# A retrieval-and-dense kernel: the product of M and Wo in three fp32r passes instead of fp32, later, with its operands split on chip

## The reference

```python
x = L0_attn_hidden_states                      # (8, 256, 512) = 16 tiles of 128 rows
xn = _layernorm(x, axis=-1)
# attention part, H 32 heads, HKV 8, D 128, G = H // HKV = 4
q = (xn @ Wq.T + bq).reshape(b, s, H, D)
sig_q = jax.nn.elu(q) + 1.0
q_sel = sig_q[:, :, ::G, :]                    # 8 of the 32 heads
num = einsum('bshd,hde->bshe', q_sel, M)
den = einsum('bshd,hd->bsh', q_sel, z)[..., None] + EPS
out_heads = jnp.repeat(num / den, G, axis=2)
output = out_heads.reshape(b, s, H * D) @ Wo.T
# dense part
out = einsum('bsd,df->bsf', xn, w.astype(float32) * w_scale) + b
x = x + output + out
```

## Time and profile before

| | |
|---|---|
| runs | 243.65 to 243.77 us, median 243.72 |
| profiled execution | 243.56 us, its span from first to last instruction 241.7 us |
| PE busy (matmuls) | 234.1 us, 97% |
| DVE, ACT, POOL busy | 178.0, 119.6, 108.4 us |
| granted clock of PE | full in all slices |
| P's products | from 57.9 to 81.8 us |

### The profile page before, as it was taken

The page is one execution under the profiler, slowest core; times in us unless marked ns, Lnnn a source line. Parts: engine busy times, 40 slices in busy tenths (PEclk is TensorE's granted clock), DMA queues, the critical chain, the costliest instruction groups (busy, mean ns, idle before and its releaser), DMA issues.

```text
span 241.7 us, 3385 instructions
## 1 busy us (share of the span) xinstructions
PE 234.1 (97%) x1030; PEld 186.7 (77%) x1030; DVE 178.0 (74%) x266; ACT 119.6 (49%) x276; POOL 108.4 (45%) x108
## 2 busy tenths in 40 slices
PE   8699999998999999999999999999999999999995
PEld 2488788885776788888888888888888888788885
DVE  2889695897998669887687694958666778995631
ACT  2654626628648923655463526455463747341110
POOL 1058734756271815553434326263403629657500
PEclk9999999999999999999999999999999999999999
DMA  7999999999370211424252515221212223244441
GB/s 225 405 417 411 383 242 225 216 217 217 94 252 5 53 51 52 127 54 126 53 168 53 161 50 169 52 91 42 88 52 73 56 75 108 76 136 136 133 174 44
DMA packets 21985, 34.83 MB, mean 144 GB/s; under 512 B 5200, under 2 KB 13136, under 8 KB 20816
## 3 DMA queue, kind: packets, MB, share of 16 engines
q1 hardware_dynamic: 19344, 26.63, 33.4%
q0 software_dynamic: 1376, 6.82, 13.4%
q10 hardware_dynamic: 1248, 1.18, 1.8%
HBM read 22.02 MB, written 4.19 MB: 108 GB/s over the span
## 4 chain that ended last, share of the span: by engine, by line
PE 33%; issue 31%; POOL 18%; DVE 8%; SPq 4%; DMA 2%; ACT 2%; ACTq 1%; POOLq 0%; DVEq 0%
POOL e_and_sz L313 9%; POOL xT L288 5%; PE attn_ps L793 4%; PE attn_ps L794 4%; PE attn_ps L795 4%; SPq L219 4%; POOL x L321 3%; PE q_ps L793 3%; PE q_ps L795 3%; PE q_ps L794 3%; DVE aT_lo L654 2%; PE dense_ps L793 2%; PE dense_ps L795 2%; PE dense_ps L794 2%; DMA xT<-in_xT 2%
## 5 line engine op out<-in xcount | busy, mean ns | idle before, releaser
L313 POOL TENSOR_TENSOR e_and_sz<-s,z_b 128x512 f32<-128x512 f32 x32 | 42.0, 1340 | 40.3 <-DVE den L633 40.2
L441 ACT ACTIVATE s<-s,rden 128x128 f32<-128x128 f32 x128 | 39.2, 389 | 40.5 <-DVE rden L637 40.5
L793 PE MATMUL attn_ps<-P_hi,aT_hi 128*128 128x512 f32 (+1 forms) x128 | 49.8, 389 | 0.5 <-DVE aT_lo L654 0.5
L795 PE MATMUL attn_ps<-P_hi,aT_lo 128*128 128x512 f32 (+1 forms) x128 | 49.1, 383 | 0.0
L794 PE MATMUL attn_ps<-P_lo,aT_hi 128*128 128x512 f32 (+1 forms) x128 | 49.0, 383 | 0.0
L793 PE MATMUL q_ps<-WqT_hi,xT_hi 128*128 128x512 f32 x104 | 42.1, 405 | 0.3 <-DVE s L628 0.3
L795 PE MATMUL q_ps<-WqT_hi,xT_lo 128*128 128x512 f32 x104 | 40.6, 390 | 0.0
L794 PE MATMUL q_ps<-WqT_lo,xT_hi 128*128 128x512 f32 x104 | 40.5, 389 | 0.0
L288 POOL TENSOR_TENSOR xT<-xT,mean_b 128x512 f32<-128x512 f32 x13 | 18.3, 1408 | 37.8 <-ACT mean_b L390 31.2
L621 DVE SCALAR_TENSOR_TENSOR q_ps<-q_ps,rstd,bq_b 128x512 f32<-128x512 f32 x28 | 21.0, 753 | 19.3 <-PE q_ps L795 19.3
L793 PEld LDWEIGHTS attn_ps<-P_hi,aT_hi 128*128 128x128 f32 x128 | 24.1, 188 | 6.2 <-issue 0.9
(11 more groups left out here) (82 smaller groups left out, 365.3 us busy)
## 6 DMA issues: line engine op xcount, KB each, us to landing
x<-in_WoT POOLq DMA_DIRECT2D x6, 1024.0 KB, 10.6
x<-in_x SPq DMA_DIRECT2D x16, 256.0 KB, 3.9
xT<-in_xT SPq DMA_DIRECT2D x16, 256.0 KB, 4.1
aT<-s SPq DMA_DIRECT2D x124, 32.0 KB, 1.9
out<-x SPq DMA_DIRECT2D x15, 256.0 KB, 2.3
MT<-s SPq DMA_DIRECT2D x96, 32.0 KB, 1.9
x<-in_WoT SPq DMA_DIRECT2D x2, 1024.0 KB, 14.0
s<-in_WqT SPq DMA_DIRECT2D x2, 512.0 KB, 7.1
```

The source lines that it names most:

```text
L313: nc.gpsimd.tensor_tensor(sz_eps[:, :, h * D // 2:(h + 1) * D // 2].rearrange("p g (j c) -> p j g c", j=2), by_quarter(sbuf_s[:, t % SRING ...
L441: last = nc.scalar.activation(a_g, a_g, ACT.Copy, scale=rden[:, t % 2, g:g + 1])
L793: nc.tensor.matmul(out, x_hi, w_hi, start=start, stop=False)
L795: return nc.tensor.matmul(out, x_lo, w_hi, start=False, stop=stop)
```

## The change

- P(g) becomes three fp32r passes. M (`MT`, 128x1024) and the eight 128x512 parts of the sum of Wo get a high part, made by ACT (`copy_M_hi`, `copy_Wo_hi(g)`), and a low part, made by DVE (`split_M_lo`, `split_Wo_lo(g)`). No space is added: M's parts lie in the second buffers of aT_hi and aT_lo, Wo's where P_hi and P_lo come to lie.
- P(g) waits for M_lo and Wo_lo(g) in place of the loads.
- PE's list: after q(5,1) now mean(7), dense(5), q(6,0), P(0), P(1), q(6,1), P(2), P(3), dense(6), P(4), mean(8); from there on unchanged.
- DVE and ACT get the new operations into their lists; the copies and splits of P, the denominators of tiles 2 and 3, the turns of tiles 1 and 3 and make_a(3) come later in them.

```diff
--- before.py
+++ after.py
@@ -85,6 +85,10 @@
         sz_eps = e_and_sz[:, E:].rearrange("p (g d) -> p g d", g=G)
         w_f32 = e_and_sz[:, 0:K * HID].rearrange("p (k n) -> p k n", n=HID)
         Wo_sum = x[:, FIRST_LENT:, :]
+        MT_hi = aT_hi[:, 1, :, :]
+        MT_lo = aT_lo[:, 1, :, :]
+        Wo_hi = P_hi
+        Wo_lo = P_lo
 
         q_ps = [bank(f"q{i}_ps") for i in range(4)]
         dense_ps = bank("dense_ps")
@@ -127,6 +131,10 @@
         wd_by_dve = sem("wd_by_dve")
         wd_hi_ready = sem("wd_hi_ready")
         wd_lo_ready = sem("wd_lo_ready")
+        M_hi_ready = sem("M_hi_ready")
+        M_lo_ready = sem("M_lo_ready")
+        Wo_hi_ready = sem("Wo_hi_ready")
+        Wo_lo_ready = sem("Wo_lo_ready")
         P_filled = sem("P_filled")
         P_hi_ready = sem("P_hi_ready")
         P_lo_ready = sem("P_lo_ready")
@@ -429,6 +437,14 @@
                 act.wait_ge(qneg_ready, 2 * t + h + 1)
                 nc.scalar.activation(e, e, ACT.Exp, scale=-1.0).then_inc(exp_ready, 1)
 
+            def copy_M_hi():
+                act.wait_ge(M_in, 16)
+                nc.scalar.activation(MT_hi, MT[:], ACT.Copy).then_inc(M_hi_ready, 1)
+
+            def copy_Wo_hi(g):
+                act.wait_ge(wo_added[g // GJ], 16 * (R - 1))
+                nc.scalar.activation(Wo_hi[:, g, :], Wo_sum[:, g, :], ACT.Copy).then_inc(Wo_hi_ready, 1)
+
             def copy_P_hi(g):
                 act.wait_ge(P_filled, g + 1)
                 nc.scalar.activation(P_hi[:, g, :], attn_ps[g % 2][:], ACT.Copy).then_inc(P_hi_ready, 1)
@@ -500,31 +516,38 @@
             copy_xT_hi(6)
             exp_of(4, 1)
             make_a(1)
+            copy_M_hi()
             exp_of(5, 0)
+            exp_of(5, 1)
+            copy_mean(7)
+            for g in range(GJ):
+                copy_Wo_hi(g)
+            exp_of(6, 0)
             copy_P_hi(0)
-            exp_of(5, 1)
             copy_P_hi(1)
-            copy_mean(7)
-            exp_of(6, 0)
+            copy_Wo_hi(4)
+            copy_Wo_hi(5)
+            copy_xT_hi(7)
+            exp_of(6, 1)
             copy_P_hi(2)
-            copy_xT_hi(7)
             copy_P_hi(3)
-            exp_of(6, 1)
+            copy_Wo_hi(6)
+            copy_Wo_hi(7)
+            copy_mean(8)
             copy_P_hi(4)
             copy_aT_hi(0)
+            copy_P_hi(5)
             make_a(2)
-            copy_mean(8)
-            copy_P_hi(5)
-            make_a(3)
             for t in range(LEAD, T):
                 exp_of(t, 0)
+                if t == LEAD:
+                    copy_P_hi(6)
+                    copy_P_hi(7)
                 if t + 1 < T:
                     copy_xT_hi(t + 1)
-                if t == LEAD:
-                    copy_P_hi(6)
                 exp_of(t, 1)
                 if t == LEAD:
-                    copy_P_hi(7)
+                    make_a(3)
                 copy_aT_hi(t - LEAD + 1)
                 if t + 2 < T:
                     copy_mean(t + 2)
@@ -606,6 +629,15 @@
                 dve.wait_ge(wd_hi_ready, j + 1)
                 nc.vector.tensor_tensor(wd_lo[:, ks, :], wd_raw[:, ks, :], wd_hi[:, ks, :].bitcast(F32), ALU.subtract
                                         ).then_inc(wd_lo_ready, 1)
+
+            def split_M_lo():
+                dve.wait_ge(M_hi_ready, 1)
+                nc.vector.tensor_tensor(MT_lo, MT[:], MT_hi.bitcast(F32), ALU.subtract).then_inc(M_lo_ready, 1)
+
+            def split_Wo_lo(g):
+                dve.wait_ge(Wo_hi_ready, g + 1)
+                nc.vector.tensor_tensor(Wo_lo[:, g, :], Wo_sum[:, g, :], Wo_hi[:, g, :].bitcast(F32), ALU.subtract
+                                        ).then_inc(Wo_lo_ready, 1)
 
             def split_P_lo(g):
                 dve.wait_ge(P_hi_ready, g + 1)
@@ -727,39 +759,46 @@
             add_dense(4)
             add_bias(5, 1)
             make_s(5, 0)
+            split_M_lo()
+            make_s(5, 1)
+            add_dense(5)
+            split_Wo_lo(0)
+            split_Wo_lo(1)
+            add_bias(6, 0)
+            turn_blocks(1)
+            split_Wo_lo(2)
+            split_Wo_lo(3)
+            make_s(6, 0)
             split_P_lo(0)
-            make_s(5, 1)
-            add_bias(6, 0)
             split_P_lo(1)
-            turn_blocks(1)
-            add_dense(5)
+            split_xT_lo(7)
+            add_bias(6, 1)
+            split_Wo_lo(4)
+            split_Wo_lo(5)
+            moments(8)
+            split_P_lo(2)
+            make_s(6, 1)
+            split_P_lo(3)
+            split_Wo_lo(6)
+            split_Wo_lo(7)
+            add_dense(6)
             denominator(2)
-            split_P_lo(2)
-            make_s(6, 0)
-            add_bias(6, 1)
-            split_xT_lo(7)
-            split_P_lo(3)
-            moments(8)
-            denominator(3)
-            add_dense(6)
-            make_s(6, 1)
             split_P_lo(4)
             split_aT_lo(0)
+            split_P_lo(5)
             turn_blocks(2)
             for t in range(LEAD, T):
                 add_bias(t, 0)
-                if t == LEAD:
-                    split_P_lo(5)
                 if t + 2 < T:
                     moments(t + 2)
                 add_bias(t, 1)
                 if t == LEAD:
                     split_P_lo(6)
-                if t == LEAD:
                     split_P_lo(7)
-                turn_blocks(t - BEHIND - 1)
+                    denominator(3)
                 if t == LEAD:
                     split_xT_lo(t + 1)
+                turn_blocks(t - BEHIND - 1)
                 make_s(t, 0)
                 if LEAD < t < T - 1:
                     split_xT_lo(t + 1)
@@ -847,14 +886,14 @@
 
             def product_P(g):
                 if g == 0:
-                    pe.wait_ge(M_in, 16)
-                pe.wait_ge(wo_added[g // GJ], 16 * (R - 1))
+                    pe.wait_ge(M_lo_ready, 1)
+                pe.wait_ge(Wo_lo_ready, g + 1)
                 if g < 2:
                     pe.wait_ge(s_ready, 9 + g)
                 else:
                     pe.wait_ge(P_lo_ready, g - 1)
-                nc.tensor.matmul(attn_ps[g % 2][:], MT[:, g, :], Wo_sum[:, g, :], start=True, stop=True
-                                 ).then_inc(P_filled, 1)
+                three_passes(attn_ps[g % 2][:], MT_hi[:, g, :], MT_lo[:, g, :], Wo_hi[:, g, :], Wo_lo[:, g, :], True, True
+                             ).then_inc(P_filled, 1)
 
             def product_attn(t):
                 if t == 0:
@@ -935,13 +974,13 @@
             product_q(5, 0)
             product_dense(4)
             product_q(5, 1)
-            product_P(0)
-            product_q(6, 0)
-            product_P(1)
             spread_mean(7)
             product_dense(5)
+            product_q(6, 0)
+            product_P(0)
+            product_P(1)
+            product_q(6, 1)
             product_P(2)
-            product_q(6, 1)
             product_P(3)
             product_dense(6)
             product_P(4)
```

## The result

The changed kernel takes 249.55 us (median of 4 runs, 249.25 to 249.99) against 243.69 for the kernel before: 1.0241 of its time, 95% interval 1.0226 to 1.0256. The profiled execution took 249.74 us with a span of 247.9, 6.2 us more than before.

What follows compares the result with a forecast made beforehand. PE was taken as the bound, busy 234.1 of 241.7 us at full clock. Terms -1.4 - 1.2 + 3.2 + 0.45 + 0.5 + 1.9 + 0.8 + 0.3 + 0.7 = +5.25 gave 248.8 us, range 245.3 to 251.3.

Steps and rivals of the forecast that it cites:

- The passes: P's eight products on PE: three fp32r passes take 0.69 instead of 0.86 us each, saving 1.4 us.
- The wait at P(0): PE's wait between q(5,1) and P(0) goes because P(0) comes 8 us later: 1.2 us saved.
- The hole: PE stands idle before dense(5), from 56.84 to 60.05, waiting for DVE's add_dense(4): 3.2 us added.
- the walk: Step-by-step timeline of ACT, DVE and PE with the new instructions moved in; denominator(2) on DVE at 77.76 (before: 66.19).
- The clock: Rival, chance 0.25: PE's clock falls to 1.2 GHz in the hole, 1.6 us more, 250.4 us.
- P(2), P(4): PE stalls 0.45 us at P(2) for P_lo(0) and 0.5 us at P(4) for P_lo(2).
- aT_lo(0) against POOL: DVE's aT_lo(0) halves meet POOL's tile 3 products, ending at 83.8 instead of 81.0; P(7) stalls 1.9 us.
- The first rival: Chance 0.2: DVE late but misses POOL, aT_lo(0) ends at 81.0 to 82.1, P(7) stalls little; +2.4, 246.0 us.
- attn(0), dense(8), mean(10): PE stalls 0.8 us at attn(0) for P_lo(6), 0.3 at dense(8), 0.7 at mean(10).
- The sum: All savings and stalls on PE together: +5.25 us on the profiled 243.56, giving 248.8; forecast's chance 0.4.
- Only the hole costs: Rival, chance 0.05: DVE takes the splits in its idle time; +0.6 us, 244.2.
- faster: Rival, chance 0.07: dense(5) finds add_dense(4) done and the splits are hidden; -2.5 us, 241.1.

Runs made afterwards that it cites:

- the kernel with the new list and the fp32 product: Reordered engine lists (PE: P(0) behind q(6,1); DVE: add_dense(4) ahead of xT(6)'s split), one fp32 product per head, no M/Wo copies or splits: 242.57 us, 0.9961 of before.
- the hole filled: Changed kernel plus 13 bf16 matmuls of zeros on PE between mean(7) and dense(5): 247.88 us, 1.0179 of the kernel before.
- the run of 242.32 us: Changed kernel with reordered PE, DVE and ACT lists, Wo splits for heads 2 to 7 on POOL behind DVE's Wo_lo(1): 242.32 us, 0.9935 of before.

## Why the prediction was right, and where not

The time lay 0.75 us above the forecast and inside its range. But two errors of over a microsecond stand in it with opposite signs, and that it came so near is luck.

- **The passes**: 0.17 us saved per head; measured 0.86 - 0.68 = 0.18. Right.
- **The wait at P(0)**: gone. Right in the changed kernel; the kernel with the new list and the fp32 product is 1.1 us faster than before, which fits the 1.2.
- **The hole**: forecast 3.2, measured 60.07 - 56.97 = 3.1, with add_dense as releaser. Right as a stall. What the text didn't see is that with DVE as late as the walk had it, the hole was no cost of its own: taken out, it came back at P(0).
- **The clock**: a rival with a chance of a quarter and 1.6 us. It happened: the trace shows it, the other three runs have the same mean clock of 0.993, and it cost 1.67. The forecast's main case left it out, and the chance was too low.
- **P(2), P(4)**: forecast 0.45 and 0.5. With the start-up of a matmul behind a wait they were 0.6 and 0.5. Right.
- **aT_lo(0) against POOL**: the step that failed, in its size. I took the 3.02 us of the earlier trace rows as an end 2.25 us behind that of POOL's products, which made 4.1 us from 79.7. Measured with the hole filled: 79.63 to 82.55, 2.92 us. DVE was let in between POOL's two products, whose pair took 3.00 instead of 2.54; the first half of aT_lo(0) was done 1.22 us after 79.63. In the earlier trace rows it came during the second one. P(7) therefore stalled 0.7 instead of 1.9, and everything behind it in the table is 1.2 to 1.4 us earlier than the walk. That the meeting would be there, and that the moves of tile 1 would hang on it, was right. The first rival named this very course, "a split that gets in between POOL's two products"; the end at 82.55 lies between its 81.0 to 82.1 and the 83.8 of the forecast.
- **attn(0), dense(8), mean(10)**: forecast 0.8, 0.3, 0.7. In the changed kernel 0.6, 0.5, 0.7. Right.
- **The sum**: with the meeting right it would have been 248.8 - 1.2 = 247.6 without the clock (measured 247.9) and 249.3 with it (249.55).

"Only the hole costs" and "faster" are refuted by the stalls at P and by the 3.4 us of the splits. The time of the changed kernel can now be told as -1.4 - 1.2 + 3.1 + 1.7 + 0.6 + 0.5 + 0.7 + 0.6 + 0.5 + 0.7 + 0.1 = +5.9, against 5.86 between the medians and 6.0 at mean(10) in the traces (104.17 - 98.18). The last 0.1 is what the trace of the changed kernel is late before anything was changed (56.64 against 56.51 at the last matmul of q(5,1)). The terms don't add as causes: the hole's 3.1 and DVE's lateness replace each other.

What stays open: behind which gap the clock falls, and for how long. The traces show it behind 2.93, 2.94 and 3.00 us, behind 2.22, behind 2.69 and 0.70, and behind 1.01 and 0.70 close together; they show it full behind 2.47 and behind 0.97. The gap alone may not decide it: two of the 17 runs of the kernel before that stand beside the run of 242.32 us also had a mean clock of 0.993 (244.84 and 245.01 us), and the trace of that kernel, of another execution, has no gap above 1.0.

## What to carry to other kernels

Before moving work of the bound engine, look at what it covers: the fp32 products stood where PE would otherwise have waited for DVE, and the wait that they had was the cheaper one. Count an added split not only by its duration on the engine but by whom it meets: here 6 us of extra DVE work with 4 us of room cost 3.4 us to save 1.4, and a meeting with POOL, which adds 1.6 us to a pair of splits, cost 1.1 with what hung on it. When a gap of the bound engine can't be avoided, it may pay to fill it with idle matmuls (1.67 us here), but one line in the order of the engine that releases it did as much.

## What the runs showed of the hardware that I had not expected

- A gap of 2.93 us on PE, in which it had nothing to do, is followed by a stretch at the lower of the two clock levels (granted 0.53 from 60 to 62 and 0.57 on average from 60 to 64 us, matmuls 0.42 us apart instead of 0.23), and it cost 1.7 us. In another execution with the same gap the clock stayed low for longer (0.50 from 60 to 64, 0.74 from 64 to 68). The Trainium skill (TensorE: Matmul & The Clock Gate, "Why this matters for your kernels") warns of such gaps; the trace agrees with the effect.
- A DVE instruction with two SBUF inputs and a POOL tensor_tensor hold each other up, but not always by as much: a pair of DVE's took 2.91 to 2.93 us where it began during the first of POOL's two products or during the second with the addition of b behind it, and 3.31 and 3.43 us beside a POOL that splits too, instead of 1.28. POOL's pair took 2.96 to 3.00 instead of 2.54. A DVE split that reads PSUM and SBUF isn't held up: P_lo(4) took 0.64 us at 80.83, beside POOL's products from 80.75. The Trainium skill (GPSIMD Engine Reference, Key points) names the contention; its size here is 1.6 to 2.2 us for a pair of 128x512 splits.
- The fp32 product of 128x512, shown as two matmuls, costs 0.86 us, 1.26 times the 0.68 of three fp32r passes. Beside the splits that they need, the passes brought nothing measurable here (242.57 and 242.56 us).
